# Rotated attention: four PSUM banks for the product with Wv Wo, and the exchange of halves moved from VectorE to ScalarE

## The reference

```python
q = (x @ q_w.T + q_b) * scale            # x: layer-normed stream
kv = x @ kv_w.T + kv_b
k, v = (kv[..., :E], kv[..., E:])
q = _rope(q)                             # per head of 128: x*cos + concat(-x2, x1)*sin
k = _rope(k)
scores = jnp.einsum('bse,bte->bst', q, k)
attn = jax.nn.softmax(scores, axis=-1)
o = jnp.einsum('bst,bte->bse', attn, v)
return o @ o_w.T
```

## Time and profile before

| | us |
|---|---|
| median of 3 runs | 3381.49 |
| lowest, highest run | 3376.54, 3390.52 |
| span of the profiled execution, first to last instruction | 3376.4 |
| the stage of the change, from SyncE's first load to the first load of the next stage | 1642.4 to 1976.6 |

### The profile page before, as it was taken

One profiled execution on the slowest core, in us unless ns is written; L12 is line 12 of the kernel. 1 busy time (PEld: TensorE's weight loads), 2 busy tenths in 40 slices (PEclk: granted clock), 3 DMA queues, 4 the chain that ended last, 5 costly groups with the idle time before them and its releaser, 6 DMA issues. The chain is left out here.

```text
span 3376.4 us, 46857 instructions
## 1 busy us (share of the span) xinstructions
PE 2992.2 (89%) x16388; PEld 2260.9 (67%) x16388; DVE 1996.1 (59%) x5348; ACT 1551.2 (46%) x3598; POOL 1019.2 (30%) x1143
## 2 busy tenths in 40 slices
PE   6999799997999977978788767998689999989999
PEld 4777678885666645446566646775467777768887
DVE  5666587775555554233747767664678777742121
ACT  5777566664666652133222244444455555531000
POOL 3655333222444530000156640000133233322222
PEclk9999899998999987988899988999799999999999
DMA  2000301101000021203100020003100000020000
GB/s 87 2 2 1 113 32 32 32 32 63 1 2 1 2 67 64 100 7 117 66 4 4 2 101 1 1 1 119 34 1 1 1 1 1 1 103 13 13 13 13
DMA packets 65872, 105.51 MB, mean 31 GB/s; under 512 B 9315, under 2 KB 29795, under 8 KB 65509
## 3 DMA queue, kind: packets, MB, share of 16 engines
q1 hardware_dynamic: 65222, 102.41, 8.7%
q0 software_dynamic: 416, 0.10, 0.0%
HBM read 89.75 MB, written 12.85 MB: 30 GB/s over the span
## 5 line engine op out<-in xcount | busy, mean ns | idle before, releaser
L714 POOL TENSOR_SCALAR a_P<-a_P,a_rec 128x512 f32<-128x512 f32 (+3 forms) x256 | 301.5, 1190 | 350.9 <-DVE a_rec L872 350.9
L402 ACT ACTIVATE tree_value<-tree_bit,table_lut,tree_step 128x256 f32<-128x256 uint8 x496 | 275.3, 595 | 140.8 <-DVE tree_value L416 73.0
L416 DVE COPY_PREDICATED tree_value<-tree_bit,tree_value 128x256 f32<-128x256 uint8 x434 | 235.0, 547 | 133.3 <-ACT tree_value L402 104.9
L787 ACT ACTIVATE a_P<-a_P,a_low 128x384 f32<-128x384 f32 (+3 forms) x512 | 281.7, 558 | 25.0 <-DVE a_low L866 24.9
L101 PE MATMUL bank<-f_xT_hi,f_w_hi 128*128 128x512 f32 (+1 forms) x704 | 276.6, 393 | 14.0 <-DVE f_w_lo L1214 14.0
L102 PE MATMUL bank<-f_xT_hi,f_w_lo 128*128 128x512 f32 (+1 forms) x704 | 276.1, 392 | 0.0
L103 PE MATMUL bank<-f_xT_lo,f_w_hi 128*128 128x512 f32 (+1 forms) x704 | 275.7, 392 | 0.0
L1136 POOL CAST f_h_hi<-f_sg 128x512 fp32r<-128x512 f32 (+1 forms) x88 | 84.5, 961 | 587.6 <-DVE f_sg L1236 297.8
L866 DVE CUSTOM_DVE_ANT_0 a_P<-bank,a_causal 128x384 f32<-128x384 f32 (+3 forms) x512 | 222.9, 482 | 63.1 <-PE bank L949 62.6
L794 ACT ACTIVATE a_PT<-bank 128x512 f32<-128x512 f32 x320 | 174.2, 594 | 83.3 <-PE bank L960 82.6
L1236 DVE TENSOR_TENSOR f_sg<-bank,f_sg 128x512 f32<-128x512 f32 (+1 forms) x44 | 30.4, 691 | 269.4 <-PE bank L103 269.4
(11 more groups left out here) (464 smaller groups left out, 7922.7 us busy)
## 6 DMA issues: line engine op xcount, KB each, us to landing
f_w_raw<-in_f_w SPq DMA_DIRECT2D x11, 768.0 KB, 12.8
f_w_raw<-table_w SPq DMA_DIRECT2D x11, 768.0 KB, 11.2
tree_idx<-in_f_idx SPq DMA_DIRECT2D x62, 128.0 KB, 2.1
table_w<-tree_value SPq DMA_DIRECT2D x62, 128.0 KB, 1.7
x_res<-in_x SPq DMA_DIRECT2D x4, 1024.0 KB, 10.8
m_piece<-in_m_wq SPq DMA_DIRECT2D x2, 2048.0 KB, 12.1
m_piece<-in_m_wo SPq DMA_DIRECT2D x2, 2048.0 KB, 8.5
m_piece<-in_m_w_gate SPq DMA_DIRECT2D x2, 2048.0 KB, 10.4
```

Source lines behind the costliest of these rows:

```text
L402: act.activation(prog.tree_value[(h + to) % 4][:, :], prog.tree_bit[h % 2][0][:, :], ACT.Identity, bias=prog.table_lut[:, 2 * k:2 * k + 1] ...
L416: dve.copy_predicated(prog.tree_value[(h + keep) % 4][:, :], prog.tree_bit[h % 2][bit][:, :], prog.tree_value[(h + other) % 4][:, :]).then ...
L714: last = pool.tensor_scalar(Pr[j][:, g, col:col + n], Pr[j][:, g, col:col + n], rec[:, j, i, g:g + 1], None, ALU.mult)
L787: last = act.activation(Pr[j][:, k, col:col + n], Pr[j][:, k, col:col + n], ACT.Exp, bias=low[:, j, i, k:k + 1], scale=-1.0, accum_out=tot ...
```

## The change

Two edits in `attention512`, and one table of constants. The four U units get the banks 3, 6, 7 and 2 in place of 2, 3, 2, 3. ScalarE, once flat n is written, makes two more copies of 64 x 512 that put its halves exchanged into a new tile `swapped[n % 2]`, and VectorE makes by_sin from that in one instruction of 128 x 512; the signs of the sine table change places with it. by_cos is still made from flat.

```diff
--- before.py
+++ after.py
@@ -1380,10 +1380,12 @@
     nm = prog.sb(name + "_nm", [P, TT], F32)
     rs = prog.sb(name + "_rs", [P, TT], F32)
     rec = prog.sb(name + "_rec", [P, TT], F32)
+    swapped = [prog.sb(f"{name}_swapped{i}", [P, T], F32) for i in range(2)]
+    c_swap = prog.count("swapped")
 
 
     QK = [(what, c) for what in ("q", "k") for c in range(DC)]
-    T_BANK, PV_BANK = (0, 1, 3, 0), (7, 2, 7, 2)
+    T_BANK, PV_BANK, U_BANK = (0, 1, 3, 0), (7, 2, 7, 2), (3, 6, 7, 2)
 
     ORDER = [("T", 0, tt) for tt in range(TT)] + [("qk", 0, i) for i in range(len(QK))]
     ORDER += [("vo", 0, c) for c in range(DC)] + [("const", 0, 0)]
@@ -1404,7 +1406,7 @@
         if b + 1 < NB:
             ORDER += [("qk", b + 1, i) for i in range(len(QK))]
 
-    BANK = {"T": lambda k: T_BANK[k], "qk": lambda k: k % 2, "vo": lambda k: 2 + k % 2, "const": lambda k: 4, "U": lambda k: 2 + k % 2,
+    BANK = {"T": lambda k: T_BANK[k], "qk": lambda k: k % 2, "vo": lambda k: 2 + k % 2, "const": lambda k: 4, "U": lambda k: U_BANK[k],
             "S": lambda k: 4 + k % 2, "PT": lambda k: 6, "PV": lambda k: PV_BANK[k]}
     J = Jobs(prog.full, prog.free, [((kind, b, k), BANK[kind](k)) for kind, b, k in ORDER])
     full, vacant, read = (lambda *key: J.full(key, 0)), (lambda *key: J.vacant(key, 0)), (lambda *key: J.read(key, 0))
@@ -1496,6 +1498,9 @@
                     else:
                         last = act.activation(flat[n % 2][:, :], bank(*key)[:, :], ACT.Identity, bias=bias[:, 1, c:c + 1])
                     last.then_inc(J.frees(key), 1)
+                    act.wait_ge(*read(*key))
+                    act.activation(swapped[n % 2][0:H, :], flat[n % 2][H:P, :], ACT.Copy)
+                    act.activation(swapped[n % 2][H:P, :], flat[n % 2][0:H, :], ACT.Copy).then_inc(c_swap.sem, 1)
                     if k:
                         finish(n - 1)
                     if k == NQK - 1:
@@ -1574,12 +1579,11 @@
                     n = b * NQK + k
                     what, c = QK[k]
                     hi, lo, whole = rope(n)
-                    dve.wait_ge(*read(*key))
+                    dve.wait_ge(*c_swap(0, n + 1))
                     if n >= 2:
                         dve.wait_ge(*c_turn(0, n - 1))
                     i = n % 2
-                    dve.tensor_tensor(by_sin[i][0:H, :], flat[i][H:P, :], trig[H:P, 1, :], ALU.mult)
-                    dve.tensor_tensor(by_sin[i][H:P, :], flat[i][0:H, :], trig[0:H, 1, :], ALU.mult).then_inc(c_sin.sem, 1)
+                    dve.tensor_tensor(by_sin[i][:, :], swapped[i][:, :], trig[:, 1, :], ALU.mult).then_inc(c_sin.sem, 1)
                     if k:
                         finish(n - 1)
                     dve.wait_ge(*c_cos(0, n + 1))
@@ -1690,7 +1694,7 @@
         w_in[i].advance(16)
     c_const.advance(32)
     for c, n in ((c_stat, NB), (c_mv, NB), (c_var, NB), (c_rstd, NB), (c_xn, NT), (c_xhi, NT), (c_shift, NT), (c_init, 2), (c_whi, 4), (c_wlo, 4),
-                 (c_vohi, DC), (c_cos, NB * NQK), (c_sin, NB * NQK), (c_turn, NB * NQK), (c_qkhi, NB * NQK), (c_qklo, NB * NQK),
+                 (c_swap, NB * NQK), (c_vohi, DC), (c_cos, NB * NQK), (c_sin, NB * NQK), (c_turn, NB * NQK), (c_qkhi, NB * NQK), (c_qklo, NB * NQK),
                  (c_uhi, NT), (c_max, NT), (c_pthi, NT), (c_rec, NT)):
         c.advance(n)
 
@@ -3298,7 +3302,7 @@
         ang = (np.arange(T, dtype=f)[:, None] * inv[None, :]).astype(f)
         out[name] = np.stack([np.cos(ang), np.sin(ang), -np.sin(ang)]).astype(f)
     cos, sin = out["c_trig128"][0].T, out["c_trig128"][1].T
-    out["c_rope128"] = np.stack([np.concatenate([cos, cos]), np.concatenate([sin, -sin])])
+    out["c_rope128"] = np.stack([np.concatenate([cos, cos]), np.concatenate([-sin, sin])])
     return out
```

## The result

The change makes the kernel faster by 0.8%. The median went from 3382.1 us (3376.54 to 3390.52, 4 runs) to 3354.06 us (3350.79 to 3355.95, 4 runs), a ratio of 0.9918 with a 95% interval of 0.9903 to 0.9933. The prediction was 3359 with a range of 3344 to 3371. The profiled execution took 3350.79 us with a span of 3348.9, which is 27.5 less than the span before; 22.5 were predicted. It was the fastest of the four.

A forecast was written before the change was run, and what follows sets the result against it. GpSimd's chain of by_cos, bo, mv and table was taken to bound the kernel. Savings reached 4.2, 9.9, 16.0 and 20.1 along the batches, 22.5 at the stage's end: 3376.4 to 3353.9, plus 5.1 gives 3359.0; range 3344 to 3371.

The forecast's parts named there:

- GpSimd's chain: by_cos 7, bo, wait for mv, table, next by_cos: ends last in every batch by about 7 us; 3359, chance 0.70.
- the table's store: Stage end: GpSimd's table becomes last, its store lands 2.0 after issue and the next load follows; stage 22.5 us shorter.
- the round: Rotation, one chunk on VectorE: 3.76 us falls to 3.15, saving 0.61 each time; bounds 3.06 and 3.30.
- ScalarE's own round: hi 0.54, flat 0.70 and two copies 1.08, together 2.32; fits in 3.15, so the copies were costed at nothing.
- The tail with `bo` and `mv`: End of a batch's rotation: lo 7 ends 0.55 after bo instead of 2.5; mv, roots and table come 2.0 earlier.
- The step from span to median: Whole kernel: the runs' median lies 5.1 above the profiled span, so 3353.9 becomes 3359.0.
- Rival C: ScalarE's copies are dear: each 0.1 us above 0.95 per copy adds 4 us; at 1.08, 3364; chance 0.08.
- Rival E: Copies make ScalarE the bound: gain used up at 1.5 us per copy, 3396 at 1.89; chance 0.04.
- Rival B: TensorE's wait is the time: all it loses comes back, some 40 us, 3341; chance 0.07.
- Rival D: The rotation's time per chunk does not shrink, through by_cos blocking or extra hops between engines: 3374; chance 0.11.
- The rule on the shared port: VectorE against GpSimd's by_cos: the loser is fully blocked for the whole instruction; read strictly, 3.30 per chunk, giving back 3 us.
- the waits of TensorE ahead of S 0 and of the first P transpose: Expected profile sign: TensorE waits 1 to 3 us at these two places, and no longer for U_lo before U 2.

The follow-up runs named there:

- the spread table: Changed kernel with one of GpSimd's four table parts done in the first batch's vo slots, the others spread over four batches: 3326.26 us, ratio 0.9843.
- the kernel with both edits: Changed kernel with GpSimd's table work partly moved into the first batch, and next-batch statistics on VectorE ahead of by_sin 0: 3330.84 us, ratio 0.9856.

## Why the prediction was right

Its frame held at each point: GpSimd's chain ends last (without the table, -23.4), TensorE's 30.7 us of waits are no measure of the gain (banks alone, 4.9), by_cos 0 stands behind the table without idle time, and the table's store lets the next stage start. The gains up to each by_cos 0, and at the table's end:

| up to | predicted | measured |
|---|---|---|
| by_cos 0, second batch | 4.2 | 4.5 |
| by_cos 0, third | 9.9 | 10.8 |
| by_cos 0, fourth | 16.0 | 17.9 |
| end of the table | 20.1 | 23.6 |
| next stage's load | 22.5 | 26.0 |

**The mis-sized term is the round**, 3.15 predicted, 3.00 measured where VectorE, GpSimd and ScalarE set it. The working took one steady loop in which each add is blocked anew. In fact ScalarE's own round of 2.54 (0.22 above my 2.32, since copies start 0.64 apart and not 0.54) makes by_sin late in every second round. In each short round the add gets in ahead of by_cos and takes 0.69; what by_cos then blocks is the start of the late by_sin, 1.12 instead of 0.68. So the exclusion costs less over the two. The sum counts five rounds per batch, and they came out shorter still, 2.93 on average (14.5 to 14.9 from flat 2 to flat 7): in the second batch three of the five are short ones, and elsewhere some rounds run at the 2.72 of a unit of TensorE. The working foresaw neither. From by_cos 0 to flat 7 the later batches took 18.2, 18.1 and 18.5 where I had 19.4, 3.4 less in all, and the first batch had gained 5.6 at hi 7 where I had 4.2. Small terms went both ways. The tail with `bo` and `mv` came as described, lo 7 ending 0.55 after `bo`, but from flat 7 to the roots it saved 1.6 and 1.7 instead of 2.0. The first batch gave 1.1 back by the next by_cos 0, of it 0.8 in the first unit of the product of Wv and Wo, which TensorE ran in 5.48 us instead of 4.71. The step from flat 7 to `bo` is 0.2 to 0.6 longer. The first table step of the last batch takes 1.15 where it was 2.09.

The sum for the stage was 3.5 too small, a little over an eighth of the gain; the forecast of the median was 4.9 too high. The step from span to median, 5.1, held by luck. Every execution whose time and span are both on record stands 1.75 to 1.92 above its span; the rest of the 5.1 came from which execution happened to be profiled, and the profiled one after was the fastest of its four, 3.3 under their median.

**Rival C** (dear copies) named 0.95 per copy as the point where the cover is gone. The copies take 0.65. Doubling them, 1.28 for each copy of the change, cost 19.8; C's formula gives 40 x (1.28 - 0.95) = 13. With the measured 2.93 for the round the cover ends at 0.85 and it gives 17; the rest is mostly flat 2 of the first batch. **Rival E** had its turning point at 1.5 per copy. The doubled kernel stands at 1.28 and is still 7.6 us under before; at C's 4 us per further 0.1, the turn would come near 1.47, an estimate. **Rival B** (all of TensorE's wait comes back) fits only once the table is out of the way: the spread table shows 3326, lower still than its 3341. B counted the shorter rounds only roughly, and no run divides up these 15 us. The Trainium skill, "Perfetto Trace Analysis", section "Identifying the Most-Contended Engine", calls the engine with the highest occupancy the most contended one, but would have TensorE's headroom judged by its weight loads and not by its busy matmuls. By matmuls that engine is TensorE, 61 of 72 us, and relieving it bought 4.9; by weight loads TensorE has 49.6 and VectorE, with 52.4, comes first. On neither reading is it GpSimd, busy for 48 of 72, which set the pace through the order of its work. This corrects the use that the prediction made of the section under B. **Rival D** is out: the round shrank by 0.76.

**The rule on the shared port.** The blocked add ended 0.55 after by_cos, as in the earlier trace rows. The Trainium skill, "SBUF — State Buffer", section "Who interferes with whom", has the first to issue keep the shared ports for its whole instruction and the other fully blocked. The trace agrees: a blocked add or by_sin ends 0.55 after by_cos wherever it started, and by_cos takes up to 1.85 instead of 1.29 when VectorE got in ahead. I had read it strictly as a round of 3.30. The trace gives 3.00, on the other side of my 3.15: not for how long one is blocked, but because only every second add pays in full.

**Of what was to be seen**, the waits of TensorE ahead of S 0 and of the first P transpose were 0.94 and 0.81 in the second batch, a little under the 1 to 3 given:

```profile
1785.95 0.50 PE L101 MATMUL bank<-a_KT_hi,a_QT_hi 128*128 128x512 f32 x1 [0.94 <-DVE a_KT_lo L1561]
...
1792.52 0.66 PE L1682 MATMUL bank<-ident,a_P 128*128 128x128 f32 x4 [0.81 <-ACT a_P L1528]
```

Not foreseen were the two waits of 4.0 for a flat. They should cost nothing, as TensorE has some 7 us to spare against GpSimd (flat 0 was 7.1 us old when by_cos 0 took it); no run takes them away alone.

Open stays why 1.5 us of the gain in the span lie outside the stage; it is within the scatter of the time ahead of it. Open too is why the kernel with both edits is 4.6 us behind the spread table in the medians, when its stage is as long. In the two traced executions it lies outside the stage, 5.2 ahead of it and 2.8 behind it.

## What to carry to other kernels

Before pricing a wait, follow the chain of every engine around one period, with what it waits for in order; an engine that is busy for two thirds can bound through the order of its work, and its slack (0.71 us here), and not the length of the wait, tells how little a cure on another engine can bring: 4.9 for 30.7 of waits. When two chains are level, changes are worth little alone and much together: banks 4.9 with the table in the way, 17.0 without. Move work that can go anywhere into a stretch where its engine is idle: that was worth as much here (23 us of the stage) as leaving it out.

## What the runs showed of the hardware

- ScalarE copies of 64 x 512 from SBUF to SBUF take 0.63 each, as long as hi with 128 x 512, and start 0.64 apart, where flat starts 0.54 after a hi; why the copies don't overlap in the same way is open. Exchanging the halves of the partitions costs nothing that shows (0.65 apart without it).
- With by_cos and a VectorE instruction side by side the delay is shared out by who starts first: by_cos takes 1.29 alone and up to 1.85 when VectorE got in ahead, by_sin 0.68 alone and 1.12 against the rest of a by_cos, the add 1.77 against a whole one.
- After waits of 4.0 us (kernel after, 1827.64) and 4.3 us (banks alone without the table, 1866.60) TensorE's next matmuls start 0.43 apart, the second one 0.59 after the first, instead of 0.23. The granted clock of these stretches was 0.50, the lower level. So such a wait costs more than its length.
